# A causal attention kernel: scores computed twice, masking and part of the row sums moved to GpSimd

## What is computed

```python
q_blhd = jnp.einsum('bld,dhk->blhk', x_bld, Wq)
latent_bll = jnp.einsum('bld,dc->blc', x_bld, Wkv_down)
k_blhd = jnp.einsum('blc,chk->blhk', latent_bll, Wk_up)
v_blhd = jnp.einsum('blc,chk->blhk', latent_bll, Wv_up)
attn = jnp.einsum('bqhd,bkhd->bhqk', q_blhd, k_blhd) / jnp.sqrt(jnp.asarray(HD, dtype=x_bld.dtype))
mask = (jnp.arange(l)[None, :] <= jnp.arange(l)[:, None])[None, None]
attn = jax.nn.softmax(jnp.where(mask, attn, neg_inf), axis=-1)
y_blhd = jnp.einsum('bhqk,bkhd->bqhd', attn, v_blhd)
return jnp.einsum('bqhd,hdo->bqo', y_blhd, Wout)
```

## Time and profile before

| what | value |
|---|---|
| runs | 3156.89, 3177.37, 3180.13 us |
| median of the runs | 3177.37 us |
| span of the profiled execution | 3176.8 us, 72083 instructions |
| own time of the profiled execution | none is listed beside its span; the median of the runs is 0.6 us above the span |
| mean granted TensorE clock | 0.892 |
| attention, first scores to last sum | 60.2 to 1219.6 us |

### The profile page before, as it was taken

One profiled execution on the slowest core, in us unless ns is written; L12 is line 12 of the kernel. 1 busy time (PEld: TensorE's weight loads), 2 busy tenths in 40 slices (PEclk: granted clock), 3 DMA queues, 4 the chain that ended last, 5 costly groups with the idle time before them and its releaser, 6 DMA issues.

```text
span 3176.8 us, 72083 instructions
## 1 busy us (share of the span) xinstructions
PE 2609.5 (82%) x26192; PEld 2113.3 (67%) x26192; DVE 2032.8 (64%) x5025; ACT 1803.5 (57%) x4422; POOL 851.3 (27%) x1042
## 2 busy tenths in 40 slices
PE   3999899999999997985886289999999978858881
PEld 2777777777777776774665266666666657757661
DVE  2766767777766776774555666676676557745555
ACT  2777777777777775552444156556555545524440
POOL 0000000000000003663555233243242316644551
PEclk9999999999999997667998699999999876659995
DMA  6322333333322321112222200000000001112225
GB/s 147 49 41 41 48 44 50 48 46 46 47 41 41 45 37 37 42 41 59 70 70 81 73 2 2 2 2 2 2 2 2 2 2 39 41 44 71 70 70 168
DMA packets 117820, 140.24 MB, mean 44 GB/s; under 512 B 21324, under 2 KB 79825, under 8 KB 117360
## 3 DMA queue, kind: packets, MB, share of 16 engines
q1 hardware_dynamic: 100592, 101.63, 17.2%
q0 software_dynamic: 16896, 34.12, 3.2%
HBM read 45.85 MB, written 40.54 MB: 27 GB/s over the span
## 4 chain that ended last, share of the span: by engine, by line
PE 45%; DVE 20%; ACT 11%; another core or an unknown queue 9%; issue 8%; DMA 4%; SPq 2%; DVEq 1%; POOL 0%; ACTq 0%; POOLq 0%
PE psum L457 5%; PE psum L426 4%; PE psum L492 4%; ACT probs L446 4%; DVE state L1714 3%; DMA qs<-q_h 3%; PE psum L1511 3%; DVE neg_max L435 2%; PE psum L1559 2%; DVE x_sb L1284 2%; PE psum L543 2%; PE psum L1125 2%; PE psum L1428 2%; PE psum L1137 2%
## 5 line engine op out<-in xcount | busy, mean ns | idle before, releaser
L446 ACT ACTIVATE probs<-psum,neg_max 128x512 f32<-128x512 f32 (+3 forms) x1024 | 540.2, 538 | 242.4 <-DVE neg_max L435 242.3
L435 DVE TENSOR_REDUCE neg_max<-psum 128x1 f32<-128x512 f32 (+3 forms) x1024 | 455.4, 481 | 42.3 <-PE psum L427 26.1
L426 PE MATMUL psum<-ls,qs 96*128 96x512 f32 (+3 forms) x1024 | 379.8, 396 | 97.7 <-ACT probs L446 82.5
L457 PE MATMUL psum<-ident,probs 128*128 128x128 f32 x2560 | 428.7, 283 | 4.7 <-ACT probs L446 0.8
L1246 POOL DMA_INDIRECT y_tok<-yb,xb x272 | 267.5, 983 | 303.3 <-DVE yb L1221 232.7
L325 POOL TENSOR_TENSOR rstd<-var_eps,half_neg 128x4 f32<-128x4 f32 x32 | 41.1, 1284 | 1097.9 <-DVE var_eps L321 1097.9
L476 DVE COPY probs_t<-psum 128x512 f32<-128x512 f32 (+1 forms) x384 | 230.2, 599 | 159.8 <-PE psum L457 151.1
L426 PEld LDWEIGHTS psum<-ls,qs 96*128 96x128 f32 x1024 | 197.4, 193 | 201.9 <-ACT probs L446 118.2
L457 PEld LDWEIGHTS psum<-ident,probs 128*128 128x128 f32 x2560 | 275.4, 144 | 30.7 <-issue 19.0
L914 POOL DMA_INDIRECT x_slot<-pay,pos_i x256 | 254.0, 992 | 135.2 <-issue 72.4
L427 PE MATMUL psum<-causal_r,ident_r 128*128 128x128 f32 x1024 | 234.6, 242 | 0.0
(11 more groups left out here) (319 smaller groups left out, 6677.1 us busy)
## 6 DMA issues: line engine op xcount, KB each, us to landing
qs<-q_h SPq DMA_DIRECT2D x128, 256.0 KB, 5.8
xb<-x_slot SPq DMA_DIRECT2D x272, 66.0 KB
qs<-q_l SPq DMA_DIRECT2D x64, 256.0 KB, 5.7
y<-y_tok SPq DMA_DIRECT2D x32, 512.0 KB, 3.6
y_tok<-yb,xb POOLq DMA_INDIRECT x272
x_sb<-in_x SPq DMA_DIRECT2D x16, 256.0 KB, 5.2
x_slot<-pay,pos_i POOLq DMA_INDIRECT x256
out<-x_sb SPq DMA_DIRECT2D x16, 256.0 KB, 2.9
```

What stands on the lines that cost most here:

```text
L426: pe.matmul(o[:, at:at + n], q, ls[par][0:3 * LD, 0:n], start=(at == 0), stop=False, skip_group_check=True)
L435: last = dve.tensor_reduce(neg_max[:, par, h, qt:qt + 1], bank[u % 3][:, at:at + (qt + 1) * P], AX.X, ALU.max, negate=True)
L446: last = act.activation(probs[:, u % 3, c], bank[u % 3][:, c], ACT.Exp, bias=neg_max[:, par, h, qt:qt + 1], accum_out=row_sum[:, par, h, q ...
L457: last = pe.transpose(bank[3 + u % 2][:, c:c + P], probs[:, u % 3, c:c + P], ident[:, :])
```

## The change

The attention is rewritten as one list of slots n, 48 per sequence, in which every engine has its steps at fixed slots. Scores are made twice.

The first scores (`max_tensor`, unit n + 2 in slot n) have no mask matmul. DVE adds the mask from SBUF and takes the row maximum in one `tensor_tensor_reduce` per tile, whose output goes back to the bank; the bank is free once that is done. Per group the maxima are split in a high and a low part, turned by PE, negated and copied by ACT, and put by one 16 KB DMA in rows 96 and 97 of `qs`; `ls` has ones there.

The second scores (`turned_tensor`, unit n - 18 in slot n) have keys on partitions (`KEY_TILES`: key block 0 with 512 queries, blocks 3 and 1 with 128 and 384, block 2 with 256) and 98 rows, so that the maximum is already subtracted. ACT writes their exp straight to `probs_t`. The probabilities are no longer turned or copied. GpSimd sets what is above the diagonal to zero, per pair of heads, and adds key blocks 1, 2 and 3 on the columns that they share. PE gets the row sums of all heads with a column of ones (`ones`) in bank 6. Values need one matmul per head and key block. y stays turned: the sums are inverted once per sequence, split, spread over the rows of each head by a matmul (`own_row`) and multiplied.

Removed are `turn_tensor`, `turned_scalar`, `turned_vector`, `y_copy_scalar`, `y_back_tensor`, `y_norm_vector`, `y_fwd_tensor`, `y_copy2_scalar`, and the double buffer of the normalized input (`xh[1]` is no longer used here; projections of the next sequence start once this one's are done). Projection, LayerNorm and `proj_sync` keep their instructions, with other slots and waits. The new functions, with their indentation cut:

```diff
+KEY_TILES = [[(0, 0)], [(3, 0), (1, 128)], [(2, 0)]]
...
+GU = HG * UNITS
+LAG = 18
+SLOTS = SEQS * UPS
+GROUPS = SEQS * G
+PAIR_U = GU // 2
...
+def max_tensor(pe, n):
+    b, u = divmod(n, UPS)
+    h, k = divmod(u, UNITS)
+    o = bank[n % 3]
+    if u % GU == 0:
+        pe.wait_ge(s["q_dma"], (n // GU + 1) * 16 * Q_DMAS)
+    if n > 2:
+        pe.wait_ge(s["s_max"], n - 2)
+    for qt, at in UNIT_TILES[k]:
+        w_q = (qt + 1) * P
+        last = pe.matmul(o[:, at:at + w_q], qs[0:3 * LD, h, qt * P:(qt + 1) * P], ls[b % 2][0:3 * LD, 0:w_q],
+                         start=(at == 0), stop=True, skip_group_check=True)
+    last.then_inc(s["s_mm"], 1)
+def max_vector(dve, n):
+    h, k = divmod(n % UPS, UNITS)
+    dve.wait_ge(s["s_mm"], n + 1)
+    for qt, at in UNIT_TILES[k]:
+        w_q = (qt + 1) * P
+        last = dve.tensor_tensor_reduce(
+            out=bank[n % 3][:, at:at + w_q], in0=bank[n % 3][:, at:at + w_q], in1=causal[:, L - w_q:L], scale=1.0,
+            scalar=-3.0e38, op0=ALU.add, op1=ALU.max,
+            accum_out=mx_raw[:, h // HG % 2, qt, h % HG:h % HG + 1])
+    last.then_inc(s["s_max"], 1)
+def max_split_vector(dve, i):
+    dve.wait_ge(s["s_max"], (i + 1) * GU)
+    if i:
+        dve.wait_ge(s["neg_t"], i)
+    dve.tensor_copy(mx2[:, :, 0, :], mx_raw[:, i % 2, :, :]).then_inc(s["mx_step"], 1)
+    dve.wait_ge(s["mx_step"], 2 * i + 1)
+    dve.tensor_tensor(mx2[:, :, 1, :], mx_raw[:, i % 2, :, :], mx2[:, :, 0, :],
+                      ALU.subtract).then_inc(s["mx_step"], 1)
+def neg_tensor(pe, i):
+    b, g = divmod(i, G)
+    pe.wait_ge(s["mx_step"], 2 * i + 2)
+    if g == 0:
+        pe.wait_ge(s["q_lo"], lo_done(b, 5))
+    elif b == SEQS - 1:
+        pe.wait_ge(s["q_lo"], lo_done(b, 6))
+    elif g == 1:
+        pe.wait_ge(s["q_lo"], lo_done(b + 1, 1))
+    else:
+        pe.wait_ge(s["q_lo"], lo_done(b + 1, g + 1))
+    if g >= 2 and b:
+        pe.wait_ge(s["x_done"], b)
+    if i:
+        pe.wait_ge(s["neg_cp"], i)
+    for t in range(QT):
+        last = pe.transpose(ln_bank[0:2 * HG, t * P:(t + 1) * P],
+                            mx2[:, t, :, :].rearrange("p s j -> p (s j)").bitcast(F32), ident[:, :])
+    last.then_inc(s["neg_t"], 1)
+def neg_scalar(act, i):
+    act.wait_ge(s["neg_t"], i + 1)
+    if i:
+        act.wait_ge(s["neg_dma"], 16 * i)
+    act.activation(neg_row[0:2 * HG, 0:L], ln_bank[0:2 * HG, :], ACT.Copy, scale=-1.0).then_inc(s["neg_cp"], 1)
+def neg_sync(sp, i):
+    b, g = divmod(i, G)
+    sp.wait_ge(s["neg_cp"], i + 1)
+    if b:
+        sp.wait_ge(s["t_mm"], (b - 1) * UPS + (g + 1) * GU)
+    sp.dma_start(qs[3 * LD:3 * LD + 2, g * HG:(g + 1) * HG, :].bitcast(F32),
+                 neg_row[0:2 * HG, 0:L].bitcast(F32)).then_inc(s["neg_dma"], 16)
+def turned_tensor(pe, m):
+    b, u = divmod(m, UPS)
+    h, k = divmod(u, UNITS)
+    o = bank[3 + m % 2]
+    if u % GU == 0:
+        pe.wait_ge(s["neg_dma"], 16 * (m // GU + 1))
+    if m > 1:
+        pe.wait_ge(s["t_exp"], m - 1)
+    for kb, at in KEY_TILES[k]:
+        last = pe.matmul(o[:, at:at + L - kb * P], ls[b % 2][0:3 * LD + 2, kb * P:(kb + 1) * P],
+                         qs[0:3 * LD + 2, h, kb * P:L], start=(at == 0), stop=True, skip_group_check=True)
+    last.then_inc(s["t_mm"], 1)
+def exp_scalar(act, m):
+    h, k = divmod(m % UPS, UNITS)
+    i = m // GU
+    act.wait_ge(s["t_mm"], m + 1)
+    if m % GU == 0 and i >= 2:
+        act.wait_ge(s["pv_mm"], i - 1)
+    act.activation(probs_t[:, i % 2, h % HG, UNIT_AT[k]:UNIT_AT[k] + UNIT_COLS[k]],
+                   bank[3 + m % 2][:, 0:UNIT_COLS[k]], ACT.Exp).then_inc(s["t_exp"], 1)
+def mask_gpsimd(pool, i, pair):
+    heads = slice(2 * pair, 2 * pair + 2)
+    n_pair = 2 * i + pair
+    p = probs_t[:, i % 2, heads, :]
+    pool.wait_ge(s["t_exp"], (n_pair + 1) * PAIR_U)
+    for at in (0, 640, 512, 1024):
+        last = pool.affine_select(out=p[:, :, at:at + P], in_=p[:, :, at:at + P], compare_op=ALU.is_ge,
+                                  fill=0.0, base=0, pattern=[[0, 2], [1, P]], channel_multiplier=-1)
+    last.then_inc(s["p_step"], 1)
+    pool.wait_ge(s["p_step"], 3 * n_pair + 1)
+    if i:
+        pool.wait_ge(s["rs_mm"], i)
+    pool.tensor_tensor(acc[:, heads, :], p[:, :, 768:1024], p[:, :, 1024:1280], ALU.add).then_inc(s["p_step"], 1)
+    pool.wait_ge(s["p_step"], 3 * n_pair + 2)
+    pool.tensor_tensor(acc[:, heads, P:2 * P], acc[:, heads, P:2 * P], p[:, :, 512:640],
+                       ALU.add).then_inc(s["p_step"], 1)
+def sums_tensor(pe, i, part):
+    b, g = divmod(i, G)
+    if part == 0:
+        pe.wait_ge(s["p_step"], 6 * i + 6)
+        if g == 0 and b:
+            pe.wait_ge(s["y_norm"], b * G)
+    for j in range(HG):
+        o = bank[6][j * LD:(j + 1) * LD, :]
+        if part == 0:
+            last = pe.matmul(o[:, :], ones[:, g, :], probs_t[:, i % 2, j, 0:L], start=(g == 0), stop=False,
+                             skip_group_check=True)
+        elif part == 1:
+            pe.matmul(o[:, P:2 * P], ones[:, g, :], probs_t[:, i % 2, j, 640:768], start=False, stop=False,
+                      skip_group_check=True)
+        else:
+            last = pe.matmul(o[:, 2 * P:L], ones[:, g, :], acc[:, j, :], start=False, stop=(g == G - 1),
+                             skip_group_check=True)
+    if part == 2:
+        last.then_inc(s["rs_mm"], 1)
+def values_tensor(pe, i, tiles):
+    b, g = divmod(i, G)
+    for kb, at in tiles:
+        if kb == 0 and i:
+            pe.wait_ge(s["y_ev"], i)
+            if g == 0:
+                pe.wait_ge(s["y_norm"], i)
+        for j in range(HG):
+            last = pe.matmul(bank[5][j * LD:(j + 1) * LD, kb * P:L], lat_tok[b % 2][:, kb, :],
+                             probs_t[:, i % 2, j, at:at + L - kb * P], start=(kb == 0), stop=(kb == QT - 1),
+                             skip_group_check=True)
+    if kb == QT - 1:
+        last.then_inc(s["pv_mm"], 1)
+def y_scalar(act, i):
+    b, g = divmod(i, G)
+    act.wait_ge(s["pv_mm"], i + 1)
+    if g == 0 and b:
+        act.wait_ge(s["o_mm"], b)
+    act.activation(y_n[:, g, :], bank[5][:, :], ACT.Copy).then_inc(s["y_ev"], 1)
+def inverse_vector(dve, b, half):
+    dve.wait_ge(s["rs_mm"], (b + 1) * G)
+    for c in (2 * half, 2 * half + 1):
+        dve.reciprocal(xn[:, c, :], bank[6][:, c * P:(c + 1) * P]).then_inc(s["r_step"], 1)
+def inverse_scalar(act, b):
+    act.wait_ge(s["r_step"], b * (QT + 1) + QT)
+    act.activation(r_h[:, :], xn[:, :, :].rearrange("p t d -> p (t d)"), ACT.Copy).then_inc(s["r_hi"], 1)
+def inverse_low_vector(dve, b):
+    dve.wait_ge(s["r_hi"], b + 1)
+    dve.tensor_tensor(r_l[:, :], xn[:, :, :].rearrange("p t d -> p (t d)"), r_h[:, :], ALU.subtract).then_inc(s["r_step"], 1)
+def spread_tensor(pe, b, g):
+    if g == 0:
+        pe.wait_ge(s["r_step"], (b + 1) * (QT + 1))
+    elif g == 1:
+        pe.wait_ge(s["y_ev"], (b + 1) * G)
+    else:
+        pe.wait_ge(s["y_norm"], b * G + g - 1)
+    o = bank[6 - g % 2][:, :]
+    pe.matmul(o, own_row[:, g, :], r_h[:, :], start=True, stop=False)
+    pe.matmul(o, own_row[:, g, :], r_l[:, :], start=False, stop=True).then_inc(s["rb_mm"], 1)
+def norm_vector(dve, b, g):
+    dve.wait_ge(s["rb_mm"], b * G + g + 1)
+    dve.wait_ge(s["y_ev"], b * G + g + 1)
+    dve.tensor_tensor(y_n[:, g, :], bank[6 - g % 2][:, :], y_n[:, g, :], ALU.mult).then_inc(s["y_norm"], 1)
+def out_tensor(pe, b, tiles):
+    if 0 in tiles:
+        pe.wait_ge(s["y_norm"], (b + 1) * G)
+        pe.wait_ge(s["neg_cp"], min((b + 1) * G + 2, GROUPS))
+        if b + 2 < SEQS:
+            pe.wait_ge(s["q_lo"], lo_done(b + 2, 3))
+    for t in tiles:
+        for g in range(G):
+            last = pe.matmul(ln_bank[:, t * P:(t + 1) * P], y_n[:, g, t * P:(t + 1) * P], wvo[:, g, :],
+                             start=(g == 0), stop=(g == G - 1))
+    if QT - 1 in tiles:
+        last.then_inc(s["o_mm"], 1)
...
+NEG_PE, NEG_ACT, NEG_SP = 13, 14, 15
+PAIR_AT = (24, 30)
+SUM_AT, PV_AT, Y_AT = 34, 36, 39
+PROJ_AT = {4: (0, 4), 16: (0, 5), 22: (1, 0), 27: (1, 1), 29: (1, 2), 40: (1, 3)}
+LN_AT = {"stats": 6, "rstd": 9, "norm": 13, "turn": 19, "hi": 20, "lo": 21}
+INV_AT, INV_HI, INV_LO, SPREAD_AT, NORM_AT, OUT_AT = 72, 74, 75, 76, 77, 81
+TAIL = OUT_AT + 4 - UPS
```

More of the change, by code:

```diff
@@ L147, in program @@
         qs = sb("qs", [P, H, L], F32R)
-        lat_hi = sb("lat_hi", [P, L], F32R)
+        probs_t = sb("probs_t", [P, 2, HG, HEAD_COLS])
+        acc = sb("acc", [P, HG, 2 * P])
+        y_n = sb("y_n", [P, G, L])
         ls = [sb(f"ls{i}", [P, L], F32R) for i in range(2)]
         lat_tok = [sb(f"lat_tok{i}", [P, QT, LD]) for i in range(2)]
[L151 to L158, removed]
+        r_h = sb("r_h", [P, L], F32R)
+        r_l = sb("r_l", [P, L], F32R)
+        causal = sb("causal", [P, L])
+        mx_raw = sb("mx_raw", [P, 2, QT, HG])
+        mx2 = sb("mx2", [P, QT, 2, HG], F32R)
+        ones = sb("ones", [P, G, LD])
         stack.close()
@@ L526, in y_fwd_tensor @@
```

(44 more changed lines are left out.)

412 lines of the change are left out of this document (140 added, 272 removed).

## The result

The changed kernel takes 3283.21 us (median of 4 runs, 3275.62 to 3285.54) against 3178.41 us before, a ratio of 1.0346 (95% interval 1.0311 to 1.0381). Forecast were 3035 us and a faster kernel; it became slower. The profiled execution has a span of 3281.1 us.

What follows compares the result with a forecast made beforehand. The bound was taken as a chain through three engines, PE nearest to full. At 62 us per sequence instead of 71.6, 16 sequences gain 154, the start 4, the end loses 16: 3176.8 - 142 = 3035 us, range 2895 to 3175.

Steps and rivals of the forecast that it cites:

- the ring: Attention before: each of three banks goes from PE's scores to DVE's maximum to ACT's exp and back; PE 77% busy.
- PE's sum: PE's work per attention sequence: 25.9 us removed, 20.8 added, so from 55.1 to 50.0 us.
- The in-place maximum: DVE's masked maximum written back to its bank: main part costs nothing extra, giving out the maximum 2.9 us per sequence.
- the pace: Attention time per sequence: PE's 50 us plus 15 for uneven slots, about 3 hidden, so 62 instead of 71.6.
- five slots in which DVE waits for ACT's copy: Projection slots of a sequence: DVE waits 0.76 us each, then subtracts for 0.6, some 5 us together.
- GpSimd's late adds: GpSimd's masking and adds before the row sums: about 0.5 us late per group where slots are light.
- the slots with reciprocals: Two slots with two reciprocals each: DVE 2.5 to 2.8 us against PE 1.5 to 1.8, costing 2 us.
- The end of the attention: After the last first scores: 31 us to the last sum instead of 15, a loss of 16 us.
- A: Attention overlap: nearly all unevenness hidden, PE alone paces, 53 us per sequence, 2891 us in all; chance 0.20.
- B: DVE's in-place maximum writes at half rate and DVE bounds: 75 us per sequence, 3243 us in all; chance 0.12.
- C: GpSimd's selects and adds late: sums wait 2 us more each group, 70 us per sequence, 3163 in all; chance 0.11.
- D: Negated maxima late: their transfer takes 4.8 us instead of 2.5, 71.2 per sequence, 3182 in all; chance 0.07.

Runs made afterwards that it cites:

- e6: Changed kernel with DVE's projection remainders one to three slots later and second scores repeated in light slots: ratio 0.9812 to the kernel before, 65.7 us a sequence.
- e3: Changed kernel with a plain maximum over the unmasked tile, no write to PSUM: ratio 1.0362 to the kernel before, 76.8 us a sequence.
- e2: Changed kernel with DVE's remainders of four projections one to three slots later: ratio 0.9998 to the kernel before, 71.4 us a sequence.
- e8: e6 with ACT's copies of projections and negated maxima before the slot's exp: ratio 0.9766 to the kernel before, 65.0 us a sequence.
- e5: e2 with ACT's copies before the slot's exp, no repeats: ratio 0.9886 to the kernel before, 70.0 us a sequence.
- e11: e8 with one of GpSimd's four selects per pair, not computing the reference: one run, 3069.89 us beside 3173.54 before, 63.4 us a sequence.
- e4: Changed kernel with one of GpSimd's four selects per pair, not computing the reference: one run, 3088.28 us beside 2998.34 before, 76.3 us a sequence.
- e9: Changed kernel with second scores repeated in light slots, six in slots 5, 17 and 41, remainders unmoved: ratio 1.058 to the kernel before, 81.9 us a sequence.
- e12: e8 with reciprocals of 8 of 128 columns, not computing the reference: one run, 2925.01 us beside 2987.07 before, 64.8 us a sequence.

## Why the prediction was wrong

**What bounds the kernel before, and the removals.** Right as far as the runs show it: ACT left the ring, and PE's and DVE's instructions went as listed. DVE's busy time per sequence fell from 50.3 to 45.8 (412.20/9), the 45.8 of the forecast. ACT came to 32.5 (292.64/9) against about 32, GpSimd to 29.0 against 27.

**PE's sum** (50.0) was too low. By the prediction's own steps slots 10 to 13, with scores, sums, values and turned maxima, take 5.7 us; in e6, at full clock, they took 6.7. Slots 36 to 38 take 4.2 by the steps and 4.9 in the trace of the changed kernel (803.36 to 808.22), with PE busy throughout. Such slots come four times a sequence, so PE's sum was short by some 4 us, an estimate from these slots.

**The in-place maximum** was priced about right. Its step for 512 columns is 0.60 us (812.01 to 812.61), as that of the plain maximum in e3, so its read costs no time of its own there, and removing all of it gained nothing (e3). For 128 columns the step is 0.25 against 0.20. The rule that the prediction cites from the Trainium skill, VectorE: DVE Perf Modes, section "Two Vector instructions with no wait between them", is that an instruction which also writes out its accumulator is two. The trace agrees: 576 reads of 140 ns, beside 576 maxima.

**The step that failed is the pace**, 50 raised to 62 by a list of uneven slots; it came to 76.8. Two terms:

- "five slots in which DVE waits for ACT's copy ... and then subtracts for 0.6, some 5". The wait was taken from L401, 0.76, a wait of the old order. (Five times 0.76 and 0.6 would be 6.8, not 5.) In the new order DVE comes to its subtraction 0.9 us before PE has ended the product, ACT then does its exp first for 0.7, as the section on the change says and the prediction doesn't price, and the copy takes 0.6. A wait is 2.3 us, 9.3 per sequence in the trace. Moving the subtraction gave back 5.4 (e2), copies first another 0.8 to 1.4 (e8, e5).
- The clock was kept at 0.97 throughout. The forecast counted PE's idle time in light slots as free, since it doesn't pace them. It isn't: behind 7.10 us in which PE was busy for 5.83, the four full slots ran at a clock of 0.55 and took 11.0 us in place of 6.7. This cost 5.7 us a sequence net of the added work (71.4 in e2, 65.7 in e6), 5.0 by the other pair, in the profiled executions, and 2.5 to 4.5 by the medians of the whole. None of the rivals had this mechanism.

Together they are 11 to 12 of the 14.8 us, which e8 gave back. How these split between the two depends on which sequences one takes. e8's 65.0 stays 3.0 above the forecast's 62. GpSimd's late adds are 1.6 of it (e11), of which the forecast had counted a part; the rest fits PE's sum, but no run tests that. The 2 us for the slots with reciprocals were right: slots 24 to 26 of the changed kernel take 7.4 us (777.06 to 784.42), with PE busy for 5.1.

**The end of the attention** was forecast at 31 us from the last first scores to the last sum; in the trace they lie at 1263.9 and 1311.7, so 48, at a mean clock of 0.79, where the 15 us of before had 1.00. **What lies behind the attention**, forecast as unchanged, took 1969.4 us against 1957.2 with the same 14880 matmuls and a clock of 0.84 both times; these 12 us aren't explained and no run was made on them. The sum: 16 x 14.8 = 237, 17 and 12 make 266 against the 246 by which the span missed (3281.1 to 3035); the first and the last sequence, which have other slots, take up the rest.

**The rivals.** A (perfect overlap) is far off. B named the right side for the wrong reason: e3. C cost 0.5 us a sequence here (e4), 1.6 in the best version. D did not come: from the issue of the negated maxima to the second scores that wait for them it is 2.3 us (808.41 to 810.73), and 0.15 to 0.35 us of waiting in that place.

## What to carry over

When several engines take turns in fixed slots, write for every wait of the new schedule what its releaser has in its own order ahead of the release, on each engine of the chain; a wait measured in the old schedule was off by a factor of three here. Work that stands behind such a wait (here the maxima behind the remainder of a projection) is what one should move first. And count TensorE's idle time at the price of the clock: here 31 redundant short matmul groups, in slots paced by another engine, made a sequence 5 to 6 us shorter in the traces and 2.5 to 4.5 over whole runs. They help only where PE would stand idle and nobody waits behind them; in front of a release they cost their full length (slot 5 of e9: 0.7 us for six). And they fill the slots, so that a later saving on another engine no longer shows there (e12).

## What the runs showed of the hardware

In e2_defer the granted clock fell to half behind stretches in which PE was busy for 5.83 of 7.10 us, with no wait for a maximum longer than 1.0 us, twice in each steady sequence and at the same slots. With those slots filled its mean between 500 and 1100 us was 1.00, in e6 and in e8. In e5_copy_first the same instructions took 73.1 us at a clock of 0.86 and 66.9 at 0.95. Four heads side by side on 32 output rows each keep their rate at 512 columns: 1.06 us for four heads of the values product (803.89), where four key blocks of 128 took 1.01 before. A select on GpSimd over 2 x 128 columns takes 409 ns, within the estimate of 0.28 to 0.50 us; an add on 512 columns takes 1274 ns, a little over the estimated 1.13 us.
